# A selective-scan layer: the C rows spread by transposes, unit 7 turned like the other odd units, units 4 and 12 with C products on GpSimd

## The reference

```python
x_dbl = jnp.einsum('bkdl,kcd->bkcl', xs, x_proj_w)      # k: 4 directions, d: 256 channels, l: 128 positions
dts, Bs, Cs = jnp.split(x_dbl, [DT_RANK, DT_RANK + D_STATE], axis=2)   # 8, 16 and 16 rows
dts = jnp.einsum('bkrl,kdr->bkdl', dts, dt_projs_w)
dts = jax.nn.softplus(dts + dt_projs_b[None, :, :, None])
def step(h, inp):
    u, dt, Bl, Cl = inp
    dA = jnp.exp(dt[..., None] * A)
    h = h * dA + (dt * u)[..., None] * Bl[:, :, None, :]
    y = jnp.einsum('bkdn,bkn->bkd', h, Cl)
    return (h, y)
```

## Time and profile before

| | us |
|---|---|
| median of 3 runs | 29268.55 (29249.78 to 29271.03) |
| the profiled execution | 29284.73 |
| its span, first to last instruction | 29282.9 |
| second layer, in it | from about 4774 on |

### The profile page before, as it was taken

The page is one execution under the profiler, slowest core; times in us unless marked ns, Lnnn a source line. Parts: engine busy times, 40 slices in busy tenths (PEclk is TensorE's granted clock), DMA queues, the critical chain, the costliest instruction groups (busy, mean ns, idle before and its releaser), DMA issues.

```text
span 29282.9 us, 495306 instructions
## 1 busy us (share of the span) xinstructions
PE 23746.5 (81%) x145198; PEld 17788.1 (61%) x145198; DVE 25685.0 (88%) x24511; ACT 23805.4 (81%) x48778; POOL 23349.3 (80%) x10372
## 2 busy tenths in 40 slices
PE   5999995888888888887888888888878888888887
PEld 1656563666666666666666666666666666666666
DVE  7555555999999999999999999999999999999999
ACT  2444444998889899888888888898888888998888
POOL 4000003999999999999999999999999999999999
PEclk6999997999999999999999999999999999999999
DMA  4000003333333333333333333333333333333333
GB/s 143 26 27 26 26 27 139 108 106 106 107 106 108 106 107 106 106 107 107 106 106 106 105 108 106 107 106 106 107 107 106 107 106 107 106 106 108 106 108 97
DMA packets 2189273, 2869.65 MB, mean 98 GB/s; under 512 B 695002, under 2 KB 964858, under 8 KB 2177786
## 3 DMA queue, kind: packets, MB, share of 16 engines
q1 hardware_dynamic: 2181978, 2803.33, 31.2%
q10 hardware_dynamic: 4608, 33.82, 0.3%
HBM read 2667.01 MB, written 169.74 MB: 97 GB/s over the span
## 4 chain that ended last, share of the span: by engine, by line
ACT 27%; PE 25%; issue 16%; DVE 11%; POOL 3%; ACTq 1%; DVEq 1%; DMA 0%; SPq 0%; POOLq 0%
DVE hst L1535 10%; PE yps L1245 8%; ACT dbT L1425 6%; ACT dAs L1403 6%; ACT dA L1403 6%; PE dbx L1230 5%; PE misc L1145 5%; PE misc L1164 2%; POOL hc L1612 2%; POOL dbu L1598 1%; DVE hc L1543 1%; ACT vab L1358 1%; PE misc L1181 1%; PE cps L1221 1%; ACT vab L1344 1%
## 5 line engine op out<-in xcount | busy, mean ns | idle before, releaser
L1598 POOL TENSOR_TENSOR dbu<-dtu,bb 128x1024 f32<-128x1024 f32 x4096 | 9686.7, 2371 | 1217.2 <-DVE hst L1535 1215.0
L1535 DVE TENSOR_TENSOR_SCAN hst<-dA,dbu 128x1024 f32<-128x1024 f32 x4096 | 9347.6, 2282 | 773.1 <-ACT dA L1403 750.2
L1612 POOL TENSOR_TENSOR hc<-hst,cc 128x1024 f32<-128x1024 f32 x4096 | 9728.0, 2375 | 5.1 <-DVE hst L1535 4.0
L1245 PE MATMUL yps<-ident,hc 128*128 128x128 f32 x65536 | 8945.1, 283 | 333.0 <-POOL hc L1612 329.7
L1245 PEld LDWEIGHTS yps<-ident,hc 128*128 128x128 f32 x65536 | 7986.0, 147 | 1823.7 <-issue 1273.3
L1535 DVE TENSOR_TENSOR_SCAN hst<-dAs,dbx 128x1024 f32<-128x1024 f32 x3584 | 8117.8, 2265 | 58.8 <-issue 57.1
L1230 PE MATMUL dbx<-ident,dbT 128*128 128x128 f32 x28672 | 4153.1, 292 | 3343.6 <-DVE hst L1535 2977.8
L1230 PEld LDWEIGHTS dbx<-ident,dbT 128*128 128x128 f32 x28672 | 3391.2, 148 | 4764.1 <-DVE hst L1535 3652.8
L1425 ACT ACTIVATE dbT<-dtuT,bT 128x256 f32<-128x256 f32 x14336 | 6126.1, 495 | 18.2
L1403 ACT ACTIVATE dA<-dtv,aneg 128x508 f32<-128x508 f32 x8192 | 5291.6, 678 | 405.6 <-DVE hst L1535 402.1
L1403 ACT ACTIVATE dAs<-dtv,aneg 128x508 f32<-128x508 f32 x7168 | 4743.5, 711 | 520.1 <-DVE hst L1535 518.1
(11 more groups left out here) (188 smaller groups left out, 28222.6 us busy)
## 6 DMA issues: line engine op xcount, KB each, us to landing
bb<-l_bscr SPq DMA_DIRECT2D x1024, 1024.0 KB, 5.7
cc<-l_bscr SPq DMA_DIRECT2D x1024, 1024.0 KB, 5.5
bx<-l_bscr SPq DMA_DIRECT2D x1024, 256.0 KB, 6.1
xg<-xgp SPq DMA_DIRECT2D x512, 85.0 KB, 2.5
xgp<-xb ACTq DMA_DIRECT2D x32, 1032.0 KB, 9.4
xt<-in_x_dram SPq DMA_DIRECT2D x128, 256.0 KB, 2.8
l_xnT<-xo SPq DMA_DIRECT2D x128, 256.0 KB, 2.0
xn<-l_xnT SPq DMA_DIRECT2D x256, 128.0 KB, 2.1
```

Source lines behind the costliest of these rows:

```text
L1245: mm = pe.matmul(yps[:, p, f * P:(f + 1) * P], hc[:, u % HB, f * 512 + p * P:f * 512 + (p + 1) * P], ident[:], is_transpose=True, start=fi ...
L1535: nc.vector.tensor_tensor_scan(hst[:, v % 4, way], decays.rearrange("p f c -> p (f c)")[:, way], inputs.rearrange("p f c -> p (f c)")[:, way],
L1598: nc.gpsimd.tensor_tensor(to, dtu[:, step % 2], row.unsqueeze(1).to_broadcast([P, 2, 512]), ALU.mult).then_inc(s_inp, 1)
L1612: nc.gpsimd.tensor_tensor(hc[:, v % HB].rearrange("p (f c) -> p f c", f=2), hst[:, v % 4].rearrange("p (f c) -> p f c", f=2), row.unsqueez ...
```

## The change

- `PLAIN_ODD` is empty: unit 7 is turned like the other odd units. `C_EVEN` is (4, 12) where it was (10,): GpSimd multiplies the even units 4 and 12 by C, VectorE six units per step.
- `bT` becomes `bcT`: the transposed x_dbl is kept with its 16 C columns as well as the 16 B columns.
- `spread_c` is four transposes of a column of `bcT`, repeated 128 times by a step of zero, where it was one bf16 matmul.
- `selc`, `nident`, `part`, the split jobs and ScalarE's casts for them are gone; `x_dbl` has 40 rows where it had 104, with C and B and dt once each.

```diff
-    PLAIN_ODD = (7,)
-    C_EVEN = (10,)
+    PLAIN_ODD = ()
+    C_EVEN = (4, 12)
...
-            JOBS[XPROJ[q] + 1] = (kind, "split", (q + 1) % 4, 1)
-            JOBS[XPROJ[q] + 2] = (kind, "split", (q + 1) % 4, 2)
...
-                    elif what == "split":
-
-                        pe.matmul(misc[0:96, :], nident[:], part[:, j[2] % 2], start=False, stop=True,
-                                  skip_group_check=True).then_inc(s_mf, 1)
...
-                def spread_c(ph, u):
+                def spread_c(u):
 
                     step = u // NST
-                    if u % NST == 0:
-                        pe.wait_ge(s_me, ph.misc(("own" if step else "pre", "split", step, 2)))
-                    pe.matmul(cps[:, :], selc[:, u % NST], part[:, u // NST % 2], start=True, stop=True).then_inc(s_cb, 1)
+                    for p in range(4):
+                        mm = pe.transpose(cps[:, p * P:(p + 1) * P],
+                                          bcT[:, step % 2, p, u % NST:u % NST + 1].to_broadcast([P, P]), ident[:])
+                    mm.then_inc(s_cb, 1)
...
-                        nc.scalar.copy(xdbl[0:104, j[2] % 2], misc[0:104, :])
-                        wait(act, s_cb, n * (NCD // 4) - NCD // 4)
-                        nc.scalar.copy(part[:, j[2] % 2], misc[0:96, :]).then_inc(s_me, 1)
-                    elif what == "split":
-
-                        r = 64 if j[3] == 1 else 32
-                        nc.scalar.copy(part[0:r, j[2] % 2], misc[0:r, :]).then_inc(s_me, 1)
+                        nc.scalar.copy(xdbl[0:DTR + 8, j[2] % 2], misc[0:DTR + 8, :]).then_inc(s_me, 1)
...
-                        nc.scalar.copy(bT[:, step % 2], cps[:].rearrange("p (w n) -> p w n", w=4)[:, :, NST:2 * NST]).then_inc(s_ce, 1)
+                        nc.scalar.copy(bcT[:, step % 2], cps[:].rearrange("p (w n) -> p w n", w=4)[:, :, 0:DTR]).then_inc(s_ce, 1)
```

57 lines of the change are left out of this document (23 added, 34 removed).

## The result

| | us |
|---|---|
| before, in the same measurement | 29269.79 (29249.78 to 29285.14) |
| after | 29993.72 (29950.98 to 30061.76) |
| ratio | 1.025, interval 1.0229 to 1.0271 |
| span of the profiled execution after | 29977.4 (before 29282.9) |

The change costs 724 us, 5.7 us in each of the 128 groups, where +0.7 was forecast. The time lies above the range and also above rival 1. The place that the prediction named, the fill of unit 7 ahead of the dt chain, and the low clock are what acts; the price of the low clock was set too low, and more places fell to it than was forecast.

The account below looks back on a forecast made before the run. VectorE was taken to set the pace, with some 1.1 ms of stalls imposed by ScalarE and TensorE. Terms summed to +0.7 us per group, 90 us in 128, less 8 for setup: 29350 us, range 28950 to 29780 us.

Parts of the forecast that it names:

- rival 1: TensorE at the low clock at pair 4 of all four steps: +5.0 us per group, 29900 us, chance 0.12.
- rival 4: The spread's repeated column loads twice as slowly, 0.44 us more per spread: 29630 us, chance 0.07.
- rival 3: VectorE's whole saved multiply is gained since softplus isn't late: 560 us go, 28700 us, chance 0.06.
- E: The end of scan 5 in a step; scan 8 was forecast at E + 7.1 or E + 8.7 us.
- The sum for 1.2 GHz: In pair 4, the time from scan 5's end to the dt result at the low clock: 4.85 us.
- (a): VectorE's softplus waits for ScalarE's vab some 512 times, 0.7 us or more each, where it was 102 times.
- (b): VectorE's multiply waits for TensorE's spread in more places than before; no size given.
- step 1: Second step of a group, units 4 to 8: low clock after a 4 to 5 us wait, +1.2 us.
- Step 2: Third step of a group, units 4 to 8: wait of about 2.2 us, clock mostly full, 0 us.
- sign (c): Fills of unit 7 take 1.1 or 2.0 us in the profile, which tells TensorE's clock.
- Step 3: Fourth step of a group, units 4 to 8: wait some 2.5 us, clock half and half, +0.1 us.
- The gain for unit 60: In the fourth step, the 0.79 us stall for the spread of unit 60 goes: -0.7 us.

Follow-up runs that it names:

- warm: The changed kernel plus twenty dummy transposes of the identity at the end of pairs 18, 34 and 50: 29379.64 us.
- fill_after_side_warm: The changed kernel, pair 4's unit 7 fill behind the sums of unit 3 and turning of x_dbl, plus twenty dummy transposes in pair 18: 29030.07 us.

## Why the prediction was wrong

**What was right.** The leader and its stalls; the 0.60 us of a spread; the repeated column at the price of others (rival 4 out); no full saving of the multiply (rival 3 out); the place, the fill of unit 7 ahead of the dt chain in pair 4; the waits ahead of the fills of unit 7 (1.4, 4.08, 2.29 and 2.00 us, where 1.2, 4 to 5, 2.2 and 2.5 were forecast); the low clock in the second step and the full one in the first (11.80 us in each group). At full clock scan 8 starts at E + 7.3 us there (11.80 less 2.20 and 2.26), 7.1 was forecast.

**The step that failed first: the price of the low clock.** The sum for 1.2 GHz, 0.05 + 1.76 + 1.58 + 0.44 + 1.02, puts two groups of transposes at the low rate and then goes on at the full one. That case came, in 42 of 90 groups, and there the forecast of the step holds: scan 8 at E + 8.8 us. In 34 of 90 the clock stays down for the whole chain: the turning is 1.06 us instead of 0.60, the dt matmul 2.07 instead of 1.02, the sums of unit 4 and the spread double too, and scan 8 is at E + 11.2 us. The other 14 lie between. Over the 90 groups scan 8 starts at E + 9.8 us. Before, too, there is a dt matmul of 1.92 us behind a wait of 2.08 us, so the trace of before had the price.

**The second: who waits.** The prediction has the spread of unit 6 complete at E + 6.2 us and hides it in the softplus' delay. Where the clock came back early it was complete at E + 6.4 us, and ScalarE's chain did end last (0.44 us for `vab`). The spread stands behind the dt matmul and another set of sums, and where the clock stayed down it was complete at E + 9.3 us: there it is the spread and no longer ScalarE's chain that ends VectorE's wait (4.87 us for `cps`, none for `vab`). Signs (a) and (b) of the prediction's list came out so: 417 softplus waits of 0.46 us on the mean, where 512 of 0.7 us or more were named, and 1143 multiply waits of 1.31 us. Together these two make step 1 +2.4 us where +1.2 was forecast.

**The third: which clock.** Step 2 was called mostly full and was low in 60 of 90 groups, +1.4 us where 0 was forecast. The prediction counted on the fill to tell the clock (sign (c)), but in steps 2 and 3 every fill of unit 7 ran at full clock and the clock fell behind it. Step 3 was called half and half, scan 8 at E + 7.9 us; it was low in 29 of 90, at 1.6 us or more each, and came out at E + 8.1 us on the mean. That it lost 0.7 us, not 0.1, lies more in the number before: E + 7.83 us was read in one group, and the mean of the 90 groups is E + 7.4 us. That warm brings steps 2 and 3 down to 12.12 and 11.88 us by work ahead of them shows the clock to be the cause there too.

**The small terms.** Step 2 from scan 40 on lost 0.65 us, where 0.1 was forecast. The group's start lost 1.2 us instead of 0.2. The gain for unit 60 was 0.2 and not 0.7 us, and scans 8 to 20 won 0.6 us where a loss of 0.2 stood. The -0.3 us for less low clock at fills 3 and 11 stood on something real: in before the fill of unit 3 ran mostly at the low clock in 64 of 90 groups and that of unit 11 in 54, in after in 19 and in none. What it was worth doesn't show by itself; the part for unit 11 lies in scans 8 to 20, and at the start of the group, with unit 3, the loss is larger than any gain. Elsewhere more was lost: the waits for scans ahead of fills rose from 2977.8 us to 3417.6, and the mean granted clock fell from 0.96 to 0.95. The prediction's terms add up to +0.7, the measured ones to +5.7.

**The rivals.** Rival 1 gave +5.0 us per group for the low clock at all four places. The clock fell at one of the four places in 17 of 90 groups, at two in 57 and at three in 16, so that rival 1's condition ("as soon as three of the four fall") seldom held. That the time is near rival 1's 29900 us is luck: fewer places fell, at a higher price each, and the group's start and step 2 from scan 40 on added 1.9 us. Still, 0.12 was little for it: the prediction itself had worked out waits of 4 to 5, 2.2 and 2.5 us ahead of the fills, and the earlier trace rows shows waits of 2.16 and 2.08 us with the low clock behind them. A mean of 0.96 over a stretch says nothing about the chain behind a wait.

The Trainium skill's sentence that transposes don't engage the full rate (TensorE: Matmul & The Clock Gate, Part 4), weighed in rival 1, doesn't hold here. Behind the wait of 4.08 us at 14962 us, shown above, TensorE did nothing but transposes, and the clock came back in them (granted 0.50 from 14964 to 14965, 0.78 from 14965 to 14966, 1.00 from 14967 to 14968). Three times twenty transposes of the identity per group lift the granted clock from 0.94 for the run (after) to 0.965 (warm), and a stretch of transposes alone is granted 1.00:

```profile
14741.76 2.35 PE L1294 MATMUL cps<-ident 128*128 128x128 f32 x20
...
14745.26 0.60 PE L1202 MATMUL cps<-ident,xdbl 128*128 128x128 f32 x4
14746.45 1.09 PE L1218 MATMUL dbx<-ident,dbT 128*128 128x128 f32 x8 [0.59 <-DVE hst L1525]
```

(fill_after_side_warm, second step, TensorE: four transposes in 0.60 us, where 1.06 us is the low clock; the granted clock from 14742 to 14744 us is 1.00.)

## What to carry over

Before work is put on an in-order engine that has slack, write down what stands behind it in the queue and who waits for that, and price the whole row at the low clock of TensorE too if a wait stands ahead of it: one fill ahead of a chain cost some 660 us more than the same fill behind two items of it. And read a number that is to be compared in many groups, not in one. A loss of this kind is often a matter of order, so before a change is dropped it is worth trying its new work one place later, and moving real work that can be done anywhere into the idle time ahead of the chain. And the value of taking an operation off an engine can lie in the buffer that it frees, not in its own length.
